# A graph network kernel: GpSimd issues its row gathers and scatters without waiting for the landing of each eight

## What is computed

```
h = relu(layernorm(x))
xh = h @ W;  a_src, a_dst = sum(xh * att_src), sum(xh * att_dst)      # 4 heads
alpha = leaky_relu(a_src[src] + a_dst[dst] + a_edge)                  # one per edge, and one self loop per node
p = exp(alpha - segment_max(alpha, dst)[dst])
out = segment_sum(xh[src] * p / segment_sum(p, dst)[dst], dst) + bias
x = x + attention2(relu(attention1(h)))
x = x + three hops of weighted neighbour sums (light)
x = x + message network(x, edge_attr_64), then three graph convolutions (gcn)
```

## Time and profile before

| | us |
|---|---|
| median of three runs | 6821.57 (6816.17 to 6831.55) |
| the profiled execution | 6840.86 |
| its span, first to last instruction | 6839.2 |
| TensorE busy | 3472.2 (51%) |
| VectorE busy | 4366.4 (64%) |
| ScalarE busy | 2792.9 (41%) |
| GpSimd busy | 3985.9 (58%), 3932 instructions |
| mean granted TensorE clock | 0.765 |
| DMA | 866.84 MB; the largest single transfer is the store of 12936 KB behind each attention |

### The profile page before, as it was taken

One profiled execution on the slowest core, in us unless ns is written; L12 is line 12 of the kernel. 1 busy time (PEld: TensorE's weight loads), 2 busy tenths in 40 slices (PEclk: granted clock), 3 DMA queues, 4 the chain that ended last, 5 costly groups with the idle time before them and its releaser, 6 DMA issues. The chain is left out here.

```text
span 6839.2 us, 77401 instructions
## 1 busy us (share of the span) xinstructions
PE 3472.2 (51%) x17298; PEld 2376.9 (35%) x17298; DVE 4366.4 (64%) x16582; ACT 2792.9 (41%) x6612; POOL 3985.9 (58%) x3932
## 2 busy tenths in 40 slices
PE   1517776204510000177777765666669995444443
PEld 1415555204510000044444433444436663433232
DVE  7379996263473466699999976766646664544332
ACT  1927784102200011266667643444436664322110
POOL 1646644676566455463654536777757643766777
PEclk9759997656755555589989888888879997566666
DMA  2226665346311644332544433444424444755333
GB/s 65 77 75 192 201 196 181 95 55 167 121 44 30 105 154 154 119 115 96 112 109 101 111 98 135 152 149 144 147 76 141 135 126 157 241 172 173 123 123 103
DMA packets 513600, 866.84 MB, mean 127 GB/s; under 512 B 110119, under 2 KB 169876, under 8 KB 512108
## 3 DMA queue, kind: packets, MB, share of 16 engines
q1 hardware_dynamic: 396683, 668.83, 30.3%
q0 software_dynamic: 116576, 194.34, 12.5%
HBM read 415.76 MB, written 459.09 MB: 128 GB/s over the span
## 5 line engine op out<-in xcount | busy, mean ns | idle before, releaser
L2738 POOL DMA_INDIRECT gcn_ring<-GT,gcn_index x588 | 589.9, 1003 | 199.1 <-issue 171.3
L1578 POOL DMA_INDIRECT light_ring<-C,light_s_u x392 | 393.5, 1004 | 313.9 <-DVE light_acc L1621 206.5
L2839 DVE SCALAR_TENSOR_TENSOR gcn_acc<-gcn_acc,cont,gcn_ring 128x128 f32<-128x128 f32 x588 | 204.3, 348 | 567.6 <-DMA gcn_ring<-GT,gcn_index 566.5
L2921 PE MATMUL gcn_psA<-ident,gcn_h 128*128 128x128 f32 x588 | 152.2, 409 | 605.7 <-DVE gcn_h L2842 605.3
L2888 ACT ACTIVATE gcn_hT<-gcn_psA 128x512 f32<-128x512 f32 x147 | 87.9, 598 | 702.9 <-PE gcn_psA L2921 702.7
L1421 ACT ACTIVATE tail_h<-tail_x,tail_nmr,tail_std 128x128 f32<-128x128 f32 x784 | 320.6, 483 | 9.8 <-DVE tail_nmr L1352 9.8
L2921 PEld LDWEIGHTS gcn_psA<-ident,gcn_h 128*128 128x128 f32 x588 | 98.1, 204 | 644.4 <-DVE gcn_h L2842 644.4
L995 POOL DMA_INDIRECT out<-source_rows_o,source_out_places x208 | 243.6, 1171 | 96.4 <-issue 50.3
L476 POOL DMA_INDIRECT gat_rows<-T,src_u x196 | 185.7, 948 | 184.3 <-POOLq L1108 75.2
L979 POOL DMA_INDIRECT source_rows_xs<-XHX,xs_places x208 | 236.8, 1138 | 93.2 <-issue 51.4
L476 POOL DMA_INDIRECT got_s<-TAB,src_u x196 | 197.0, 1005 | 160.5 <-DMA got_s<-TAB,src_u 63.7
(11 more groups left out here) (589 smaller groups left out, 13621.5 us busy)
## 6 DMA issues: line engine op xcount, KB each, us to landing
T<-front_t SPq DMA_DIRECT2D x196, 272.0 KB
source_rows_c<-C SPq DMA_DIRECT2D x156, 256.0 KB
GT<-source_rows_r SPq DMA_DIRECT2D x156, 256.0 KB, 2.4
C<-light_acc SPq DMA_DIRECT2D x147, 256.0 KB
gcn_own<-GT SPq DMA_DIRECT2D x147, 256.0 KB
RC<-gcn_own SPq DMA_DIRECT2D x147, 256.0 KB
gat_rows_r<-RG SPq DMA_DIRECT2D x104, 264.0 KB
RG<-gat_rows SPq DMA_DIRECT2D x2, 12936.0 KB
```

Of the source, the lines that this page charges most:

```text
L1578: nc.gpsimd.indirect_dma_start(out=ring[:, n % RING, j, :], out_offset=None, in_=tables[h], in_offset=bass.IndirectOffsetOnAxis(ap=index[: ...
L2738: nc.gpsimd.indirect_dma_start(out=ring[:, n % RING, j, :], out_offset=None, in_=net.GT[i], in_offset=bass.IndirectOffsetOnAxis(ap=index[: ...
L2839: nc.vector.scalar_tensor_tensor(out=acc[:, n % 2, j, :], in0=before, scalar=net.cont[:, c:c + 1], in1=ring[:, n % RING, j, :], op0=ALU.mu ...
L2921: ins = nc.tensor.transpose(psA[n % 2][:, j * P:(j + 1) * P], h[:, n % 2, j, :], net.ident[:, :])
```

## The change

The parameter `landed` and BATCH go, and with them the wait ahead of every further eight in four stretches; in the fifth, the wait in the middle of each half of the ring goes. The waits for all landings at the end of a stretch, and those for the stores of the ring, stay. No instruction is added or moved.

```diff
@@ -465,23 +465,16 @@
                 nc.tensor.matmul(ps[:, 0:1], net.earlier[:, :], r[:, 0:1, 0], start=True, stop=True).then_inc(r_carried, 1)
 
 
-BATCH = 8
-
-
-def gather_static(nc, table, index, out, arrived, columns=range(T), landed=None):
-
-    for i, c in enumerate(columns):
-        if landed is not None and i and i % BATCH == 0:
-            nc.gpsimd.wait_ge(arrived, 16 * (landed + i))
+def gather_static(nc, table, index, out, arrived, columns=range(T)):
+
+    for c in columns:
         nc.gpsimd.indirect_dma_start(out=out[:, c, :], out_offset=None, in_=table,
                                      in_offset=bass.IndirectOffsetOnAxis(ap=index[:, c:c + 1], axis=0)).then_inc(arrived, 16)
 
 
-def scatter_static(nc, table, index, rows, done, columns=range(T), landed=None):
-
-    for i, c in enumerate(columns):
-        if landed is not None and i and i % BATCH == 0:
-            nc.gpsimd.wait_ge(done, 16 * (landed + i))
+def scatter_static(nc, table, index, rows, done, columns=range(T)):
+
+    for c in columns:
         nc.gpsimd.indirect_dma_start(out=table, out_offset=bass.IndirectOffsetOnAxis(ap=index[:, c:c + 1], axis=0),
                                      in_=rows[:, c, :], in_offset=None, bounds_check=EP - 1, oob_is_err=False).then_inc(done, 16)
 
@@ -498,8 +491,6 @@
             pool.wait_ge(stored[k % 2], 16 * (k // 2))
         for u in range(U):
             c = k * U + u
-            if u == U // 2:
-                pool.wait_ge(arrived[k % 2], 16 * (U * (k // 2) + u))
             nc.gpsimd.indirect_dma_start(out=ring[:, k % 2, u, :], out_offset=None, in_=table,
                                          in_offset=bass.IndirectOffsetOnAxis(ap=index[:, c:c + 1], axis=0)).then_inc(arrived[k % 2], 16)
         if k >= 1:
@@ -1675,8 +1666,8 @@
                          lambda pool: fetch_target_rows(nc, net, pool, inp["x"], dst_u, xd_ring, xd_arrived, xd_stored))
 
         def look_up_both(pool):
-            gather_static(nc, net.TAB, src_u, got_s, looked_s, landed=0)
-            gather_static(nc, net.TAB, dst_u, got_d, looked_d, range(LOOKUPS_IN_FRONT), landed=0)
+            gather_static(nc, net.TAB, src_u, got_s, looked_s)
+            gather_static(nc, net.TAB, dst_u, got_d, looked_d, range(LOOKUPS_IN_FRONT))
             pool.wait_ge(looked_s, 16 * T)
         phase_front(nc, net, inp, "front", 0, NODE_GROUPS, look_up_both)
 
@@ -1684,7 +1675,7 @@
             Y = sb("gat1_rows", [P, T, WA])
 
             def fetch_sources(pool):
-                gather_static(nc, net.T1, src_u, Y, rows1_in, landed=0)
+                gather_static(nc, net.T1, src_u, Y, rows1_in)
                 pool.wait_ge(rows1_in, 16 * T)
             phase_own_projection(nc, net, fetch_sources)
 
@@ -1699,7 +1690,7 @@
             phase_attend(nc, net, 0, Y, look_up)
 
         def move_rest(pool):
-            scatter_static(nc, net.J1, place, packed, moved, range(FIRST_MOVES_BEFORE_ENDS, T), landed=FIRST_MOVES_BEFORE_ENDS)
+            scatter_static(nc, net.J1, place, packed, moved, range(FIRST_MOVES_BEFORE_ENDS, T))
             pool.wait_ge(moved, 16 * T)
             pool.dma_start(items[:, :, :], as_columns(net.J1)).then_inc(turned_back, 16)
             pool.wait_ge(turned_back, 16)
@@ -1709,7 +1700,7 @@
             Y = sb("gat2_rows", [P, T, WA])
 
             def fetch_rows(pool):
-                gather_static(nc, net.T2, q_u, Y, rows2_in, landed=0)
+                gather_static(nc, net.T2, q_u, Y, rows2_in)
                 pool.wait_ge(rows2_in, 16 * T)
             phase_high_digit(nc, net, items, place, fetch_rows)
             phase_attend(nc, net, 1, Y, lambda pool: scatter_static(nc, net.J2, place, items, moved2, range(MOVES_BEFORE_ENDS)))
```

## The result

| | before | after |
|---|---|---|
| median of four runs, us | 6825.5 (6816.2 to 6831.6) | 6713.1 (6709.1 to 6726.4) |
| span of the profiled execution | 6839.2 | 6712.0 |
| TensorE busy | 3472.2 | 3460.8 |
| VectorE busy | 4366.4 | 4357.6 |
| ScalarE busy | 2792.9 | 2792.5 |

The ratio is 0.984, with a 95% interval of 0.9821 to 0.9858: 97 to 122 us less. The forecast was 125 us less, 6697 us, in a range of 6680 to 6742.

The account below looks back on a forecast made before the run. The prediction took GpSimd, last to leave three stretches, as what bounds them. Its terms, -46.1 - 41.7 - 37 = -125 us, taken from the median of 6821.6, gave 6697 us, in a range of 6680 to 6742.

Parts of the forecast that it names:

- the two covered ones: Front look-ups and target rows: zero gain, as VectorE covers them, with 75 us and 39 us to spare.
- Own projection: Gather of source rows, GpSimd last: 24 waits of 53.3 us removed, less 0.30 us each, -46.1 us.
- High digit: Gather of the second attention's rows: 39.2 us less waiting, 2 us given back beside VectorE's work, -37 us.
- Moves behind the first attention: Scatters in gat1_rows: 16 waits removed, 42.7 us, less 1 us for the last landing, -41.7 us.
- a slower last landing: In gat1_rows, the last scatters' landing may take longer than 1.45 us of idle; 1 us taken off.
- The carry-over to the median: The profiled execution was 19 us slower than the median, 6821.6; the forecast subtracted the gain from that median.
- the best case: In the three stretches, every wait is pure latency, worth its length less 0.30 us.
- the bound of piled-up work: Worse case: waiting beyond 1.9 us is work still to be done; 64 waits worth 1.6 us each, 102 us.
- A: Rival: SyncE's streams become the last in gat1_rows, whose whole term could be lost, 6739 us; chance 0.07.
- 12 us of cover: In gat1_rows, the predicted margin left between SyncE's last store and GpSimd's new end, some 12 us.
- B: Rival: GpSimd's queue fills, removed waits return as longer issues, about 6822 us; chance 0.05, including a mixture with A.
- C: Rival: transfers pile up and hamper one another in the three stretches, 50 us slower, 6872 us; chance 0.04.

Follow-up runs that it names:

- the shift: The changed kernel with LOOKUPS_IN_FRONT at 196 in place of 98 and FIRST_MOVES_BEFORE_ENDS at 140 in place of 60: 6673.0 us, 0.9778 of before.
- the fastest kernel: The shift with MOVES_BEFORE_ENDS at 138 in place of 100 and FIRST_MOVES_BEFORE_ENDS at 131 in place of 140: 6616.3 us, 0.9699 of before.

## Why the prediction was right, and where it was off

*The number.* 125 us less was forecast and 112 measured (97 to 122): right in kind and place, and some 13 us too much. Of these, 7 are the mis-sized term below; the other 5, between the 117.8 us of the stages and the 112 of the medians, are within the medians' interval.

*Which stages count.* Right in all five. The three stages ended by GpSimd moved, the two covered ones did not, by the two kernels that took each kind alone.

*Own projection*, predicted -46.1, measured -46.05. Together the waits gave back their length less 0.30 us each. That it fits to 0.1 us is luck: against the kernel that dropped only the covered waits, the same stage is 46.8 us shorter.

*High digit*, predicted -37, measured -37.6. The gathers that now fall beside VectorE's work did take longer, 1.4 us in all (a mean of 1.022 us and not 1.015), where 2 were forecast. Here too a profile's 2 us stand against the closeness of the sum.

*Moves behind the first attention*, predicted -41.7, measured -34.2. This is the term that was mis-sized. The waits are gone as reckoned, 42.7 us; two things took 8.4 back, and the prediction had both at nothing.

The first is the time of an issue beside VectorE's work, 4.5 us. The prediction priced this for the high digit and left it out here. The windows hold the stage's scatters alone: up to VectorE's last instruction in the stage, then behind it, first before, then after (us, busy us of GpSimd and transfers, granted clock, DMA share, GB/s).

```profile
1607.70:1787.20 179.50, 113.64 (x98) 0.84 0.73 235
...
1787.20:1845.00 57.80, 36.92 (x38) 0.59 0.08 21
...
1561.70:1739.00 177.30, 135.61 (x116) 0.85 0.75 238
...
1739.00:1765.00 26.00, 19.45 (x20) 0.70 0.15 45
```

While VectorE works, an issue takes 1.16 us before and 1.17 after; once it has ended, 0.97 in both. Without the waits 18 more of the 136 scatters fall into the first part: 18 x 0.19 and 116 x 0.01 us make the 4.5. That VectorE is the cause, and not the DMA engines, was not tested by a run of its own, but the 60 scatters beside the 12.9 MB store, with VectorE idle, took 0.97 us each, and in the high digit before, with the DMA share at 0.20 and 0.21, a gather took 1.09 us beside VectorE and 0.94 alone. Nor does all of VectorE's work do it: beside that of own projection a gather takes 0.95 us, and 0.94 alone.

The second is the gap in GpSimd's issues, once in the stage: 2.95 us before, 6.80 after. Here it is in the kernel before:

```profile
1812.43 0.97 POOL L485 DMA_INDIRECT J<-packed,sort_place  x1 [2.95 <-issue]
```

Before, the gap came at 1812, when SyncE's streams had ended. Now it comes at 1734, when they are in full course. It is the same place of the queue: ahead of the 114th of the stage's 136 scatters, in before and after and in the four experiments that leave the split of the work as it was. Nor is it a matter of scatters: ahead of the 114th gather of own projection and of the high digit there is one in every kernel, 3.4 to 4.0 us, and 2.4 and 2.2 with the waits two batches back. In gat1_rows its sizes are 2.95 in all three kernels in which the streams were over, and 6.80, 5.26 and 2.37 beside them; in the first attention, beside the 12.9 MB store, 9.8 to 10.5. That suggests that what the DMA engines do makes it longer, but the 2.37, and the 3.4 us beside the streams of own projection, show that this is not all. What GpSimd does in it was not tested.

The microsecond that I took off for a slower last landing was not there: 1.45 us both times.

*The carry-over to the median.* The profiled run of before was 15 to 19 us slower than the medians, and I subtracted a gain from the median as if that part stayed. That was sound: 6825.5 - 117.8 = 6708, and 6713 was measured. The first median, 6821.6, was 4 us low, which brings the 13 us of the difference to the 16 between 6697 and 6713.

*What a missing wait could cost.* I took the best case, latency alone, against the bound of piled-up work (102 us in all). Waiting two batches back, and waiting after each four, both show latency alone, and the stages gave 117.8 us.

*The rivals.* A did not happen: SyncE's last store was issued at 1728.19 + 22.00 = 1750.2, before at 1797.6, and GpSimd's load of the items at 1765.94, and the next stage's first gather came 23 us behind that store, where I had reckoned 12 us for the stage. SyncE's stream did not grow; from the stage's first scatter to that store it takes 188.4 us, before 189.9. It becomes the last only once 80 scatters are taken out of the stage, as the shift shows. What the prediction counted as 12 us of cover was 23 because the stage gave back 8 us less than reckoned. B did not happen: the issues did not become longer in own projection (a mean of 0.95 us both times), where 196 went out with nothing to hold them. C did not happen; two batches back bounds what is in flight to 16, and takes as long.

## What to carry to other kernels

Here a wait after each batch cost the latency of one landing, with a batch of eight as with one of four, and it cost it only where the waiting engine was the last to leave a stage. Either drop it or let it look one batch further back; both gave all there was to have. Then look at where the waits were covered: that time is now free on the engine, and moving work into it was worth 40 us more. The other 57 us, down to the fastest kernel, came from a wait in the second attention that the kernel before has too, and from trimming; how much they would give beside the old waits was not run.

## What the runs showed that was not expected

GpSimd's issues have a gap of their own at a fixed place of a stage, ahead of its 114th transfer in own projection, gat1_rows and the high digit alike, whatever the number of waits: 2 to 4 us in own projection and the high digit, up to 6.8 in gat1_rows, and up to 10.5 us in an attention, beside its large store. A change that moves work in time can move such a gap into a worse place. And an engine that waits 197 us in a stage can still be on its path: 38 scatters taken from gat2_rows shortened it by 47 + 10.8 = 58 us, 1.5 us each.
